# A graph network's row gathers: a written-out loop, a ring of 32 tiles, and sums a half ahead of the mixes

## The reference, cut to what matters

```python
hs = h[src]                                   # one row for each edge
m  = sum_r (etype == r) * (hs @ W_r)          # 8 relations
h  = relu(segment_sum(m, dst) + h @ loop_w + bias) (+ h) (+ x)
```

```python
agg = segment_sum(x[col] * w, row) / clip(deg, 1)
x   = layernorm(x + concat([x, agg]) @ W.T + b)
```

## Time and profile before

| | us |
|---|---|
| median of three runs | 10056.5 |
| span of the profiled execution | 10051.3 |
| the execution's time beyond the span, as the median of the runs has it | 5.2 |
| POOL busy | 6634.6 |
| PE busy | 5458.7 |
| DVE busy | 3264.1 |
| ACT busy | 1333.7 |

### The profile page before, as it was taken

One profiled execution on the slowest core, in us unless ns is written; L12 is line 12 of the kernel. 1 busy time (PEld: TensorE's weight loads), 2 busy tenths in 40 slices (PEclk: granted clock), 3 DMA queues, 4 the chain that ended last, 5 costly groups with the idle time before them and its releaser, 6 DMA issues.

```text
span 10051.3 us, 123328 instructions
## 1 busy us (share of the span) xinstructions
PE 5458.7 (54%) x27756; PEld 4999.2 (50%) x27757; DVE 3264.1 (32%) x16373; ACT 1333.7 (13%) x3586; POOL 6634.6 (66%) x5897
## 2 busy tenths in 40 slices
PE   4444444444444444667766544444544446766665
PEld 4444444444444444566666444444444445666664
DVE  3222233222333333433333322222233334333333
ACT  1110111111111111111111211101111111111112
POOL 5555555655555556688888665565565566888887
PEclk7776676666766766555555667666777776555556
DMA  2222211111111111455555511111111113555556
GB/s 88 64 63 63 64 56 42 44 43 44 45 41 43 44 43 44 73 75 75 74 75 75 104 41 43 44 44 43 44 42 43 43 44 66 74 75 75 75 75 111
DMA packets 578839, 594.70 MB, mean 59 GB/s; under 512 B 128465, under 2 KB 470718, under 8 KB 578494
## 3 DMA queue, kind: packets, MB, share of 16 engines
q0 software_dynamic: 373312, 383.17, 23.0%
q1 hardware_dynamic: 170246, 190.65, 6.6%
q10 hardware_dynamic: 35192, 19.90, 0.7%
HBM read 431.39 MB, written 161.82 MB: 59 GB/s over the span
## 4 chain that ended last, share of the span: by engine, by line
another core or an unknown queue 34%; issue 18%; DMA 14%; POOL 13%; PE 12%; DVE 3%; ACT 3%; DVEq 2%; ACTq 2%; POOLq 0%; SPq 0%
DMA share<-scat,place 13%; POOL share L479 13%; PE msg L789 9%; PE sum L782 2%; ACT sums L592 2%; DVE acc L988 1%; DVE onehot L975 1%; PE lin L734 1%; DVEq L988 0%; ACTq L125 0%; DVEq L975 0%; DVEq L981 0%; ACTq L123 0%; ACT idx L597 0%
## 5 line engine op out<-in xcount | busy, mean ns | idle before, releaser
L511 POOL DMA_INDIRECT rows_in<-h_table,idx x3328 | 3167.2, 952 | 2196.3 <-ACT idx L597 1163.7
L479 POOL DMA_INDIRECT share<-scat,place x1664 | 2599.3, 1562 | 580.6 <-issue 323.8
L789 PE MATMUL msg<-sums,mix_w 128*128 128x128 f32 x4992 | 1128.2, 417 | 2019.1 <-ACT sums L592 992.7
L789 PEld LDWEIGHTS msg<-sums,mix_w 128*128 128x128 f32 x4992 | 1045.7, 319 | 2083.7 <-issue 1500.9
L988 DVE TENSOR_TENSOR acc<-msg,acc 128x16 f32 x4160 | 728.3, 175 | 4145.9 <-remote 1943.3
L814 PE MATMUL msg<-rows_in,sums 16*128 16x128 f32 x3328 | 1267.7, 482 | 901.2 <-ACT sums L609 899.1
L789 PE MATMUL msg<-sums,rel_w 128*128 128x128 f32 x3328 | 752.1, 417 | 1359.9 <-ACT sums L592 623.2
L789 PEld LDWEIGHTS msg<-sums,rel_w 128*128 128x128 f32 x3328 | 697.4, 319 | 1401.8 <-issue 923.2
L814 PEld LDWEIGHTS msg<-rows_in,sums 16*128 16x128 f32 x3328 | 880.9, 322 | 989.2 <-issue 500.6
L782 PE MATMUL sum<-onehot,rows_in 128*128 128x128 f32 x8320 | 1283.1, 317 | 119.1 <-issue 86.3
L592 ACT ACTIVATE sums<-sum 128x512 f32<-128x512 f32 x1040 | 602.4, 596 | 5502.3 <-remote 3618.6
(11 more groups left out here) (143 smaller groups left out, 2295.2 us busy)
## 6 DMA issues: line engine op xcount, KB each, us to landing
edges_i<-in_src_dram SPq DMA_DIRECT2D x210, 512.0 KB
rows_in<-h_table,idx POOLq DMA_INDIRECT x3328
share<-zeros SPq DMA_DIRECT2D x104, 258.0 KB
rows_in<-h_table SPq DMA_DIRECT2D x1664, 8.0 KB
share<-scat,place POOLq DMA_INDIRECT x1664
hT<-share SPq DMA_DIRECT2D x80, 258.0 KB, 4.6
h_table<-rows ACTq DMA_DIRECT2D x65, 256.0 KB
rows_in<-in_x_dram,idx POOLq DMA_INDIRECT x832
```

The source lines that it names most:

```text
L479: nc.gpsimd.indirect_dma_start(out=shares[m][a], out_offset=bass.IndirectOffsetOnAxis(ap=place[:, q // 2, 4 * (q % 2) + a:4 * (q % 2) + a ...
L511: nc.gpsimd.indirect_dma_start(out=rows_in[:, s, :], out_offset=None, in_=rows_of[:, :], in_offset=bass.IndirectOffsetOnAxis(ap=idx[:, h, ...
L789: last = nc.tensor.matmul(MSG[h][:, 0:HALF * WIN], W[:, n, :], sums[:, h, n, :, :].rearrange("p t v -> p (t v)"), start=(n == 0), stop=(n ...
```

## The change

- `idx`, its copies by ACT and the semaphores `idx_ready` go. The gathers read their row numbers from the table `srcT_i` itself, a column for each tile. For that POOL's loop over rounds is written out: 832 gathers for each layer stand in the program.
- The gathers get a ring of 32 slots, `gather_in`, made of the memory of `rows_in` and of `scat`, which the relational layers don't use. Four gathers share a semaphore: `gathered` are 8, one for each quad of the ring.
- Rounds are 32 tiles, 26 in a layer. `onehot` keeps 16 slots, so two halves.
- PE sums half `g` and then mixes half `g - 1`; at a round's end it mixes the last half as well.
- The semaphores of the single quads and halves become one each (`summed`, `evacuated`, `onehot_ready`, `messaged`).

The core of the diff (L numbers of the changed kernel are some lines off):

```diff
+DEEP = 4 * HALF
+ROUNDS = TILES // DEEP
+HALVES = TILES // HALF
@@ buffers
-        idx = sb("idx", [D, 2, HALF], I32)
-        rows_in = sb("rows_in", [D, RING, D])
+        ring = sb("ring", [D, RING * D + RING * COLS])
+        rows_in = ring[:, 0:RING * D].rearrange("p (s d) -> p s d", d=D)
+        gather_in = ring[:, 0:DEEP * D].rearrange("p (s d) -> p s d", d=D)
-        scat = sb("scat", [D, RING, COLS])
+        scat = ring[:, RING * D:].rearrange("p (s c) -> p s c", c=COLS)
@@ POOL
+            pool.wait_ge(src_in, 16)
-                    with pool.Fori(0, TURNS) as i:
-                        k = pool.snap(count(P, p, r, i))
-                        for h in range(2):
-                            pool.wait_ge(idx_ready[h], k + 1)
-                            pool.wait_ge(summed[2 * h + 1], k + 1)
-                            apart(pool)
-                            for s in range(HALF * h, HALF * (h + 1)):
-                                nc.gpsimd.indirect_dma_start(
-                                    out=rows_in[:, s, :], out_offset=None, in_=rows_of[:, :],
-                                    in_offset=bass.IndirectOffsetOnAxis(ap=idx[:, h, s % HALF:s % HALF + 1], axis=0),
-                                ).then_inc(gathered[s], 16)
+                    half = pool.snap(P * (r * HALVES) + p * HALVES)
+                    for g in range(HALVES):
+                        pool.wait_ge(summed, half * 2 + (2 * g + 2))
+                        apart(pool)
+                        for t in range(HALF * g, HALF * (g + 1)):
+                            nc.gpsimd.indirect_dma_start(
+                                out=gather_in[:, t % DEEP, :], out_offset=None, in_=rows_of[:, :],
+                                in_offset=bass.IndirectOffsetOnAxis(ap=srcT_i[:, t:t + 1], axis=0),
+                            ).then_inc(gathered[t % DEEP // 4], 16)
@@ ACT
-                                act.wait_ge(summed[q], k + 1 + q % 2)
...
-                            act.activation(idx[:, h, :], srcT[:, bass.ds((i + 1) * RING + h * HALF, HALF)],
-                                           ACT.Copy).then_inc(idx_ready[h], 1)
+                    def evacuate(i, half):
+                        for g in range(4):
+                            b = g % 2
+                            act.wait_ge(messaged, half + (g + 1))
+                            for q in range(2):
+                                act.wait_ge(summed, half * 2 + (2 * g + q + 9))
...
@@ PE (`summed` starts at 8, `messaged` and `evacuated` at 2)
+                        def sum_rows(g):
+                            for q in range(2):
+                                pe.wait_ge(onehot_ready, half * 2 + (2 * g + q + 1))
+                                pe.wait_ge(evacuated, half * 2 + (2 * g + q + 1))
+                                pe.wait_ge(gathered[2 * g + q], i * 64 + (GATHER_PASS * r + 64))
                                 for t in range(4):
...
+                        def mix_rows(g):
+                            pe.wait_ge(evacuated, half * 2 + (2 * g + 4))
+                            pe.wait_ge(added, half * HALF + (HALF * g + HALF))
...
+                        sum_rows(0)
+                        for g in range(1, 4):
+                            sum_rows(g)
+                            mix_rows(g - 1)
+                        mix_rows(3)
@@ DVE
-                        onehots(1, i, k)
-                        adds(0, i, k)
-                        with dve.If(i < TURNS - 1):
+                        onehots(1, i, half)
+                        onehots(2, i, half)
+                        adds(0, i, half)
+                        onehots(3, i, half)
+                        adds(1, i, half)
+                        with dve.If(i < ROUNDS - 1):
...
+                        adds(2, i, half)
+                        adds(3, i, half)
```

More of the change, by code:

```diff
@@ L111, in edge_passes @@
                 opened(p)
-            with eng.Fori(0, TURNS) as i:
-                turn(i, eng.snap(P * (before * TURNS) + p * TURNS + i))
+            with eng.Fori(0, ROUNDS) as i:
+                turn(i, eng.snap(P * (before * HALVES) + p * HALVES + i * 4))
             if moved:
@@ L121, in rounds @@
     def rounds(c):
-        start = eng.value_load(round_end[0:1, bass.ds(c, 1)], min_val=0, max_val=TURNS)
-        end = eng.value_load(round_end[0:1, bass.ds(c + 1, 1)], min_val=0, max_val=TURNS)
+        start = eng.value_load(round_end[0:1, bass.ds(c, 1)], min_val=0, max_val=ROUNDS)
+        end = eng.value_load(round_end[0:1, bass.ds(c + 1, 1)], min_val=0, max_val=ROUNDS)
         with eng.If(start < end):
             with eng.Fori(0, end - start) as n:
-                i = nc.s_assert_within(start + n, min_val=0, max_val=TURNS - 1,
-                                       skip_runtime_bounds_check_because="rounds before end, which is TURNS at most")
-                turn(i, eng.snap(P * (before * TURNS) + more * TURNS + i))
+                i = nc.s_assert_within(start + n, min_val=0, max_val=ROUNDS - 1,
+                                       skip_runtime_bounds_check_because="rounds before end, which is ROUNDS at most")
+                turn(i, eng.snap(P * (before * HALVES) + more * HALVES + i * 4))
         return end
@@ L272, in build @@
         passes_set = sem("passes_set")
-        idx_ready = [sem(f"idx_ready{h}") for h in range(2)]
-        gathered = [sem(f"gathered{s}") for s in range(RING)]
-        onehot_ready = [sem(f"onehot_ready{q}") for q in range(4)]
-        summed = [sem(f"summed{q}") for q in range(4)]
-        evacuated = [sem(f"evacuated{q}") for q in range(4)]
-        messaged = [sem(f"messaged{h}") for h in range(2)]
+        gathered = [sem(f"gathered{q}") for q in range(DEEP // 4)]
+        onehot_ready = sem("onehot_ready")
+        summed = sem("summed")
+        evacuated = sem("evacuated")
+        messaged = sem("messaged")
         added = sem("added")
@@ L529, in _ @@
         def _(act):
[L530 to L531 removed]
+            act.sem_inc(evacuated, 2)
             for q in range(4):
@@ L550, in _ @@
             act.activation(srcT[:, :], srcT_i, ACT.Copy).then_inc(src_cast, 1)
-            act.wait_ge(src_cast, 1)
-            for h in range(2):
-                act.activation(idx[:, h, :], srcT[:, HALF * h:HALF * (h + 1)], ACT.Copy).then_inc(idx_ready[h], 1)
             for n, (tile, banks) in enumerate(((keyT, SUM), (offT, MSG))):
@@ L687, in _ @@
         def _(pe):
-            for q in (1, 3):
-                pe.sem_inc(summed[q], 1)
-            for h in range(2):
-                pe.sem_inc(messaged[h], 1)
+            pe.sem_inc(summed, 8)
+            pe.sem_inc(messaged, 2)
             for q in (1, 3):
@@ L773, in opened, with messages @@
                         apart(pe)
[L775 to L787 removed]
+                    def messages(i, half):
+                        def sum_rows(g):
[3 more added lines that the diff above has]
+                                pe.wait_ge(gathered[2 * g + q], i * 64 + (GATHER_PASS * r + 64))
+                                for t in range(4):
+                                    last = nc.tensor.matmul(SUM[q][:, t * KEYS:(t + 1) * KEYS], gather_in[:, HALF * g + 4 * q + t, :],
+                                                            onehot[:, HALF * (g % 2) + 4 * q + t, :], start=True, stop=True)
+                                last.then_inc(summed, 1)
+                        def mix_rows(g):
+                            pe.wait_ge(evacuated, half * 2 + (2 * g + 4))
+                            pe.wait_ge(added, half * HALF + (HALF * g + HALF))
@@ L1024, in opened, with turn @@
                     def opened(p):
-                        onehots(0, 0, dve.snap(count(P, p, r, 0)))
+                        onehots(0, 0, dve.snap(P * (r * HALVES) + p * HALVES))
                         dve.wait_ge(acc_set, 2 + CHUNKS * (r + 1))
-                    def turn(i, k):
-                        onehots(1, i, k)
-                        adds(0, i, k)
-                        with dve.If(i < TURNS - 1):
-                            onehots(0, nc.s_assert_within(i + 1, min_val=1, max_val=TURNS - 1,
-                                                          skip_runtime_bounds_check_because="the condition above"), k + 1)
-                        adds(1, i, k)
+                    def turn(i, half):
+                        onehots(1, i, half)
[4 more added lines that the diff above has]
+                        with dve.If(i < ROUNDS - 1):
+                            onehots(0, nc.s_assert_within(i + 1, min_val=1, max_val=ROUNDS - 1,
+                                                          skip_runtime_bounds_check_because="the condition above"), half + 4)
+                        adds(2, i, half)
+                        adds(3, i, half)
                     def moved(p):
@@ L1100, in columns @@
                 def columns(c, j, end):
```

(2 more changed lines are left out.)

64 lines of the change are left out of this document (22 added, 42 removed).

## The result

The changed kernel takes 9808.12 us (median of 4 runs, 9803.57 to 9811.84), the kernel before 10055.53 (10054.03 to 10066.57). The ratio is 0.9753 with a 95% interval of 0.974 to 0.9767: 2.5% faster, where 6.5% was forecast. The profiled execution's span fell by 245.0 us. These rows of its page, and the DMA view's instruction queues, answer to the earlier trace rows.

A forecast was written before the change was run, and what follows sets the result against it. POOL's gathers and their waits in five relational layers were taken as the bound: 6622.4 us become 5973 at 11.5 us a half, 649 less; 10051.3 - 649 + 5 = 9407, rounded to 9400 us, range 8640 to 10000.

The forecast's parts named there:

- the index copy's place in the chain: Between released half and next gather in relational layers: evacuation 0.60 and copy 0.20 us, 0.8 us in all, would go.
- The ring of 32 lets POOL run three halves ahead: POOL's gathers: with delays covered, POOL would never wait; by this alone 12.75 us a half would become 10.05.
- the prediction's own sign: POOL in the profile after: the mechanism is wrong if POOL still pauses 2 us a half.
- The open term: How fast signals get through when gathers never pause: between 10.05 and about 11.5 us a half; 11.5 was taken.
- Sums ahead of mixes: PE's order: mixes cover the next sums' evacuations; PE's half stays at 5.7 to 6.2 us, below 10.05.
- Layer ends: PE's work after a layer's last gather: 0 to 15 us more a layer, 0 to 75 in all; 0 taken.
- Mean layers: The two layers with the scatters of L479, untouched by the change: stretches stay at 1615 and 1641 us.
- Instruction fetch: Rival, chance 0.07: doubled DVE and PE loop bodies are loaded anew, adding 600 us: 10000 us; otherwise 150 to 250 packets.
- Busy times: PE, ACT and DVE in the profile after: unchanged but for 106 us of copies.
- The coupled lag: Rival, chance 0.15: sums are released only when gathers drain, only the restart shortens: 12.3 us a half, 9820 us.
- Starvation by the deeper ring: Rival, chance 0.12: PE's and DVE's signals come only when gathers stop, which gets rarer: 14.1 us a half, 10757 us.
- POOL-bound: Rival, chance 0.30: the deep ring hides all delays, gathers run back to back: 10.05 us a half, 8655 us.

The follow-up runs named there:

- ring16_mix_after_sums: Changed kernel with 16 tiles in flight or unread instead of 32, and PE mixing each half right after its sums: 9814.29 us, 0.975 of the kernel before.
- uncoupled: Changed kernel, but PE multiplies a resident buffer without waiting for gathers, and POOL gathers without waiting for sums: 12003.55 us, 1.1941 of the kernel before.
- uncoupled_spaced: The uncoupled kernel with a clear of 128 columns and a wait for it behind every gather on POOL: 11748.2 us, 1.1691 of the kernel before.

## Why the prediction was wrong, step by step

- What bounds the kernel, and the index copy's place in the chain: right. The step from evacuation to gather fell by the 0.8 us (1.52 to 0.77) and bought 0.5 us a half (12.24 with ring16_mix_after_sums), and that was the whole gain.
- "The ring of 32 lets POOL run three halves ahead", and the delay of 6 to 14 us "is then shorter than the 30 us of work that POOL has in hand": this failed. It took the delay as a length that a longer run can cover. The runs showed a delay that grows with the run: 6.2 us after eight gathers, 15.3 after sixteen, and in the uncoupled kernel 436 of some 3300 matmuls in 1140 us. A deeper ring lengthens the run, not the cover, and with 16 slots the time was the same. By the prediction's own sign, POOL's pauses of 2.2 us a half, the mechanism was wrong. I counted by place in a run how many instructions PE began until the next gather: in the changed kernel 8.8 to 14.3 in the mean behind each of the first seven, 3.1 behind the ninth, 1.0 behind the fifteenth (weight loads counted too; a half of PE's work has some 63; a run ends with a pause of over 1 us).
- The open term, 11.5 us a half, measured 12.14. I read 11.46 and 11.54 as a rate because two places agreed, but both left out the restart: the time from delivery to the next gather. Of the 401 us between 9808 and the sum's 9407 this term is 332 (0.64 x 519.4).
- Sums ahead of mixes: priced at nothing as to the bound, and worth nothing (0.977 without, 0.9753 with, intervals overlapping).
- Layer ends: I took 0 and kept 75; they cost 70 us, the rest of the 401. Of these 48 are the deeper ring's: with the ring of 16 the five stretches behind a last gather are 28.5, 30.4, 1676.4, 24.6 and 1672.0 us.
- Mean layers, taken over: right. The second one's scatters started over 1550.5 us before (8421.0 to 9971.5) and over 1552.0 now:

```profile
L483 POOL DMA_INDIRECT share<-ring,place x832: 1554/1554/1686, 8173.3 to 9725.3; - x167
```

- Instruction fetch: 259 packets where I said 150 to 250, and not thousands. A relational layer has 40 to 48 of them (13 to 17 before); one for each round of each of the two doubled bodies would be 52 alone, beside those of POOL's written-out program. So the loops are not fetched anew, and the warning of the Trainium skill, "Runtime: NRT & Kernel Launch", Instruction fetch mechanics, that a taken branch out of the window must wait for its page, didn't come into it.
- Busy times: DVE's as said; ACT's fell by 54 us where I said 106, since copies overlapped evacuations (1621.30 and 1621.79); PE's fell by 148 us with the same 27756 instructions, where I said unchanged. As its ends are modelled, nothing is built on this.
- Rivals. The coupled lag at 12.3 us a half and 9820 us, to which I gave 0.15, is nearest to what happened, and ring16_mix_after_sums, at 12.24 us a half and a restart shorter by 0.75 us, shows its mechanism. Its "for" was stronger than I weighed: releases close behind the last gather in three places, one counterexample at 752.62, seven gathers into its run. Starvation by the deeper ring had the cause and missed the outcome: it counted a run of 32 in which nothing is done, while of 340 runs 188 went past eight gathers and seven past sixteen, and behind the first seven gathers of each PE works near its own pace (63 instructions in 5.9 us are 13 in 1.25). POOL-bound needs a delay that hides, and there is none. That the coupled lag's number fits to 12 us is in part luck: its half was to be 12.3 us and is 12.14, which is 83 us less, and the layer ends, which it had at nothing, give 70 back.
- The view that would have told: the one-hots early and late in the timeline. I looked at when signals came and not at how fast engines began their instructions.

```profile
1610.74 2.16 DVE L975 TENSOR_SCALAR onehot<-iota_ps,keyT 128x128 f32<-128x128 f32 x8 [0.63 <-issue]
...
1618.38 0.35 DVE L975 TENSOR_SCALAR onehot<-iota_ps,keyT 128x128 f32<-128x128 f32 x1 [0.59 <-issue]
```

A rule that bears on this is in the Trainium skill, "SBUF — State Buffer", SBUF: two separate sides: of the engines only DVE and GpSimd share a port pair, and PE and ACT never wait on anyone there. The measurement doesn't speak against this as a rule on ports, since ACT's evacuations took 592 to 598 ns with and without dense gathers; but as grounds for expecting gathers and matmuls to run beside each other undisturbed it fails here, by 436 matmuls in 1140 us (uncoupled) against 3338 in 640 us (uncoupled_spaced).

What stays open: what of a gather holds the others back, POOL's work on it, its start or its completion signals. Rows and bytes are ruled out; these three were not told apart. When PE's starts fall is open too, and it isn't the place in the run alone. In the kernel before, 102 runs have exactly sixteen gathers; in them PE begins 0.3 and 1.4 instructions behind the sixth and seventh gather, when it has done a half, but 9.6 to 13.3 behind each of the eighth to the twelfth, where it has the next half to do (the 16 matmuls at 756.96). A PE that has stood still for some gathers thus starts at its own pace again, deep in a run. A queue that fills, or something that an engine's pause restores, would both do it; neither is shown. Spacings between 1.25 and 1.86 us a gather, all equal, were not tried.

## What to carry to other kernels

Before you deepen a buffer to hide a delay, find out whether the delay keeps its length when the producer runs longer: take the same group of instructions early and late in a run. If "issue" gaps grow on engines that wait for nothing, the producer is in the way. Here pausing it (1.3%) and giving another engine fewer and larger instructions (0.5%) gained what depth did not, and depth paid a little (0.4%) only after that. To find it, let the two sides run uncoupled and count what the consumers get done.

## What the hardware showed unexpectedly

- Indirect gathers issued without a pause, 1.25 to 1.40 us apart, hold PE in the mean to about one instruction per gather (423 matmuls and 421 weight loads in 1040 us), at 128 or 64 rows and 512 or 256 bytes alike; spaced to 2 us they cost the other engines nothing that shows (619 us a layer against 615).
- POOL itself drops from 1.25 to 1.40 us a gather after some 200 without a rest.
- A clear of one column (0.11 us) between two gathers leaves their step at 1.25 us; waiting for its own signal adds 0.61 us.
